# Local maxima by head groups, their queries in two transfers; a token turn one score later; half of the output product by token halves

## The chip, the cores and the metric

One Trainium2 chip, one of its cores. The metric is the device time of one execution of the whole kernel in microseconds; a kernel's time is the median of its runs. The names of the engines are those of the profile: PE (TensorE, matrix products; PEld is its loading of weights), ACT (ScalarE), DVE (VectorE), POOL (GpSimd), and SP (SyncE), which here issues the transfers. SPq is SP's queue of transfers.

## What is computed

The input is x of 8 batches x 1024 tokens x 256 channels. It is normalized over the channels (no weights), and two branches of it are added to x:

```
xn  = layernorm(x)
out = x + attention(xn) + ffn(xn)

attention: q, k, v = xn @ w_qkv + b_qkv, 16 heads of 16 channels
           heads 0..3:  causal softmax over all earlier tokens
           heads 4..15: causal softmax over the last 64 tokens
           @ w_out + b_out
ffn:       Q = xn @ W_Q.T, K = xn @ W_K.T, invQ = Q @ W_inv.T, invK = K @ W_inv.T
           branch(Q, K) + alpha * branch(invQ, invK), then @ W_O.T
branch:    per expert e of 8:  (Q @ V_e) * cumsum_over_tokens(K @ W_e)
           times the softmax weight of e (a router: gelu layer, then 8 logits)
           @ U_e, + weights @ b, / (token number)
```

All inputs are float32. The kernel splits a float32 operand into a high and a low part (names ending in H and L) and multiplies three pairs, or into three bfloat16 parts for the scores.

## The kernel before

**Chunks.** The 8192 tokens are worked in 16 chunks of 512 (two to a batch; c = ch % 2 is the half of the batch). Each chunk goes through these stages on PE:

1. *Maxima and experts.* The softmax is stabilized by the greatest score of each query. Twelve local products (L865, one for each of 4 token blocks t and 3 groups of 4 heads) and 10 (c = 0) or 26 (c = 1) global ones (L879) give scores to DVE, which takes the maxima. They are woven, four at a time, into the eight expert steps: x (L731, into bank 2), c (L731, into bank 3), the products on ACT, DVE and POOL, and mix (L843), which gathers the output in banks 0 and 1. `open` (L808) starts that sum with the gate rows WT.
2. *Local attention*, `local_groups`: six units (3 head groups x 2 halves) of scores (L899, lscore), exponentials on ACT, masks on POOL, and values (L924, lav). Beside them the next chunk's tokens are turned (L749, `turn`, banks 2 and 3) and its keys, queries (parts) and hidden layer computed.
3. *Global attention*: 6 tiles (c = 0) or 14 tiles (c = 1) of scores (L938, gscore, two for each tile), exponentials (ACT L1134), masks on the diagonal (POOL L1582), and values (L958, gav). Between them stand side stages: the next chunk's gates, its values (L731 with XH as the weights, 12 products each), and `finish` (ch, 0), the first half of the output product (L969, 12 products).

An odd chunk (c = 1) therefore follows a short global stage, an even one a long stage.

**Order.** A `Plan` lists all stages once, and each engine's program walks the same list, in order, and issues its own part of each stage behind the semaphore waits. Moving a stage in the list moves it on every engine, SP's transfers included.

**The stacks.** Keys and queries are written to DRAM in three bfloat16 parts (`parts_d`) and read back in the order of the products (`STACK`: 48 rows of partitions and three times 16): KL and QS[4:] for local heads, KG and QS[0:4] for global ones. The queries' local stacks are read by stage "stacks", ch, "queries", half: with half 0 the first three of `STACK` (L1684; 576, 192 and 192 KB), with half 1 the fourth (192 KB). L865 waits for all eight local transfers of a chunk (keys and queries) by one semaphore, `local_in`. After the global stage stage "stacks", ch, "global" (L1686) reads eight transfers of 192 and 64 KB, which L879 waits for (`global_in`).

**SP's order around a chunk's start.** `add_gate_parts` lists it: gate weights to DRAM (L1724), queries half 0, wide 0 (L1760: the gate weights of an expert pair spread over the partitions, two transfers), queries half 1, the gate rows (L1733, four transfers, weight_parts), wide 1, wide 2, and the WT rows read back (L1742, three, weight_rows; they wait until the gate rows have landed). Behind it come Vs (L1695 to L1698), the global stacks, and wide 3 and later. POOL's L1600 multiplies by a wide (weigh), DVE's L1386 by c (product), which frees bank 3; ACT's L1108 and POOL's L1605 split the result for mix (PH, PL).

Of the kernel before, what the change touches and what calls it, by code (L numbers as in the profile page):

```python
# [69 lines left out]
def mixer_layer(  # L70
# [87 lines left out]
    def peak_use():  # L158
        turns["peak"] += 1
        return f"bank{(4, 5, 6, 7)[turns['peak'] % 4]}"  # L160
# [130 lines left out]
    def add_finish(ch, k):  # L291
        add("finish", ch, k, uses=[f"phl{k}"])

    def add_residual(ch):
        add("residual", ch)

# [12 lines left out]
    def add_wide(ch, j):  # L309
        add("wide", ch, j, uses=[f"wide{j % WIDE}"])  # L310

    def add_gate_parts(ch):
        add("gate_parts", ch)
        if ch:
            add("stacks", ch, "queries", 0)
        add_wide(ch, 0)
        if ch:
            add("stacks", ch, "queries", 1)
        add("weight_parts", ch)
        for j in range(1, WIDE):  # L320
            add_wide(ch, j)
        add("weight_rows", ch)

    def add_gates(ch):
# [10 lines left out]

    def peak_groups(ch):
        c = ch % NC
        order = [[(add_lpeak, ch, t, grp, peak_use())] for t in range(T) for grp in range(NL // 4)]
        gpeaks = [[(add_gpeak, ch, t, j, peak_use())] for t in range(T) for j in range(c * T + t + 1)]
        masks = [[] for _ in order + gpeaks]  # L340
        for n, ((stage, *key),) in enumerate(order + gpeaks):
            if stage is add_lpeak:
                masks[n].append((add_seed if n >= PEAKS else add_mask, key[-1], "lpeak", *key[:-1]))
            elif stage is add_gpeak and key[2] == c * T + key[1]:
                masks[n].append((add_seed, key[-1], "gpeak", *key[:-1]))
        order[-1].append((add, "found", ch, 0))
        gpeaks[2].append((add_rows, ch, 0))
        gpeaks[-1].append((add, "found", ch, 1))
        order += gpeaks
        if ch == 0:  # L350
            add_norm(1, order)
            for t in range(T):
                order[-1].append((add, "scale", 1, t))
        blocks = range(0, len(order), PEAKS)
        joined = lambda groups, n: [stage for group in groups[n:n + PEAKS] for stage in group]
        blocks = [joined(order, n) + joined(masks, n + PEAKS) for n in blocks]
        blocks[0] = joined(masks, 0) + blocks[0]
        return blocks
# [57 lines left out]
    for ch in range(CHUNKS):  # L416
# [14 lines left out]

        last_mix = [(add_mix, ch, 2 * KB - 1, part) for part in range(2)]
        if nxt:
            for k in range(DB):
                add_turn(ch + 1, k)
            side = [last_mix] + [[(add_parts, ch + 1, w, b)] for w in (1, 0) for b in range(DB)]
            side[1].append((add_rows, ch, 1))
            side += [[(add_hidden, ch + 1, 0)] + [(add, "sums", ch + 1, k) for k in range(DB)]]
            if ch + 2 < CHUNKS:
                side[-1].append((add, "load", ch + 2))  # L440
        else:
            side = experts[split:] + [last_mix]
            side[0] = side[0] + [(add_rows, ch, 1)]
        weave(local_groups(ch), side)
        scores, values = global_groups(ch)
        if not nxt:
            run(scores[0][0] + scores[0][1])
# [8 lines left out]
        if nxt:  # L456
            first_x, first_c = ([(add, ch + 1, 0, part) for part in range(2)] for add in (add_x, add_c))
            run(first_x + scores[0][0] + scores[0][1] + first_c)
            add("logits", ch + 1, uses=["bank7"])
            add("chigh", ch, 0)  # L460
            if ch + 2 < CHUNKS:
                add_norm(ch + 2, values)
            side = [[(add_gates, ch + 1), (add, "crest", ch, 0)], [(add_gate_parts, ch + 1)]] + [[]] * (3 * (ch % NC))
            side += [[(add_values, ch + 1, 0)], [(add_values, ch + 1, 1)], [(add_finish, ch, 0)]]
        else:
            side = [[(add, "chigh", ch, 0), (add, "crest", ch, 0)], [(add_finish, ch, 0)]]

# [31 lines left out]
    with ctx:  # L499
# [130 lines left out]
        peak_in = [sem(f"peak_in{i}") for i in range(2)]  # L630
        raw_in = [sem(f"raw_in{i}") for i in range(5)]
        tok_done, turned, xhi, xlo, carried, chi, clo = (sem(n) for n in ("tok_done", "turned", "xhi", "xlo", "carried", "chi", "clo"))
        parts_ps, part1, part3, local_in, global_in, kept = (sem(n) for n in ("parts_ps", "part1", "part3", "local_in", "global_in", "kept"))
        values_ps, vs_in, vs_zero, hidden_ps = (sem(n) for n in ("values_ps", "vs_in", "vs_zero", "hidden_ps"))
        gate_max, gate_exp, rows_cast, rows_out, rows_in, opened = (
            sem(n) for n in ("gate_max", "gate_exp", "rows_cast", "rows_out", "rows_in", "opened"))
# [88 lines left out]
        def tensor_program(e):  # L725
# [12 lines left out]
            for stage in plan.stages:  # L738
# [115 lines left out]
                elif kind == "lpeak":  # L854
                    ch, t, grp = key
                    i, = where[stage]
                    q.wait_ge(local_in, 128 * (ch + 1))
                    q.wait_ge(kept, ch + 1)
                    if stage in laid:
                        q.wait_ge(seeded, nth("seed", *stage))  # L860
# [102 lines left out]

                elif kind == "finish":
                    ch, k = key[:2]
                    q.wait_ge(ctx_lo, nth("crest", *key))
                    for t in range(T) if key[2:] == () else range(2 * key[2], 2 * key[2] + 2):
                        for a, b in ((PH, OH), (PH, OL), (PL, OH)):
                            ins = e.matmul(out_half(t), a[:, k, t * P:(t + 1) * P], b[:, k, :], start=False,  # L969
# [59 lines left out]
        def scalar_program(e):  # L1029
            q = Seq(e)  # L1030

            for stage in plan.stages:
# [67 lines left out]
                elif kind == "product":  # L1100
# [3 lines left out]
                    if j >= 2:  # L1104
                        q.wait_ge(phl_read[h], use(f"phl{h}", "mix", ch, j - 2, 1))
                    elif ch:
                        q.wait_ge(phl_read[h], use(f"phl{h}", "finish", ch - 1, h))
                    e.activation(PH[:, h, :], prod[:, j % 3, :], ACT.Copy).then_inc(phi)  # L1108

                elif kind == "seed":  # L1110
# [498 lines left out]
        def sync_program(e):  # L1609
# [5 lines left out]
            for stage in plan.stages:  # L1615
# [40 lines left out]
                elif kind == "parts_out":  # L1656
                    ch, w = key
                    q.wait_ge(part1, nth("parts", ch, w, DB - 1))
                    q.wait_ge(part3, nth("parts", ch, w, DB - 1))
                    q.wait_ge(local_in, 128 * ch)  # L1660
                    q.wait_ge(global_in, 128 * ch)
                    e.dma_start(parts_d[w].rearrange("(b p) i t -> p i b t", p=P), parts[:, w, :, :, :]).then_inc(parts_out[w], 16)

                elif kind == "stacks":
# [10 lines left out]
                    for w in (0,) if reach == "queries" else (1,) if reach == "local" and ch else (1, 0):  # L1675
                        q.wait_ge(parts_out[w], 16 * (ch + 1))
                        by_head = parts_d[w].rearrange("(h d) i t -> d i h t", d=HD)
                        for rows, i in STACK if half is None else (STACK[:3], STACK[3:])[half]:
                            if i is None:
                                src = parts_d[w].rearrange("(h d) i t -> (d i) h t", d=HD)  # L1680
                            else:
                                src = by_head[:, i[1 - w], :, :]
                            if reach != "global":
                                e.dma_start(KL[rows, :, WINDOW:] if w else QS[rows, NG:, :], src[:, NG:, :]).then_inc(local_in, 16)  # L1684
                            else:
                                e.dma_start(KG[rows, :, c * C:(c + 1) * C] if w else QS[rows, 0:NG, :], src[:, 0:NG, :]).then_inc(global_in, 16)  # L1686

# [71 lines left out]
                        n = 2 * (j % KB) + k  # L1759
                        e.dma_start(wide[j % WIDE][R * k:R * (k + 1), :].rearrange("p (h t) -> p h t", h=2), by_half[n:n + 1].to_broadcast([R, 2, HALF])).then_inc(wide_in[j % WIDE], 16)  # L1760

                elif kind == "finish" and key[2:]:
                    ch, _, h = key
                    q.wait_ge(bank_read[h], use(f"bank{h}", "open", ch))
                    e.dma_start(outr[ch // NC, ch % NC, :, 2 * h:2 * h + 2], xt[:, 2 * h:2 * h + 2, :]).then_inc(stored, 16)
# [43 lines left out]
```

## Time and profile before

| | before |
|---|---|
| median of 3 runs | 1412.46 us (1409.79 to 1415.1) |
| the profiled execution | 1412.41 us |
| its span, first to last instruction | 1410.7 us |
| mean granted TensorE clock | 0.993 |
| busy share of the span | PE 96%, DVE 70%, ACT 55%, POOL 42% |
| PE's first instruction | at 11.8 us |

The span is what the trace covers; the execution's own time is 1.7 us more. In the lists by time a row gives the start, the busy time of a run of equal instructions, the engine, the line and the operation as output<-inputs, how many (x), and in brackets the idle time of the engine before it with what ended it. The waits list sums such idle time by the instruction that waited and by what it waited for.

### The profile page before, as it was taken

The numbers are of one execution on the slowest core, as the hardware profiler recorded it, in microseconds if no ns is written. First come the engines' busy times: TensorE is split into PE (matmuls) and PEld (weight loads), VectorE is DVE, ScalarE is ACT, GpSimd is POOL, SyncE is SP. The second block draws the span as 40 slices with busy tenths as digits, with TensorE's granted clock in tenths as the row PEclk, the third lists the DMA queues.
The fourth block names the chain that finished last, engine by engine and source line by source line (L and its number), as shares of the span: only waits on it lengthen the run. The fifth ranks groups of instructions, "written<-read, shape, count | busy, mean of one in ns | idle before, by whom it ended". The sixth has DMA issues, their size and how long they took to land.

```text
span 1410.7 us, 35955 instructions
## 1 busy us (share of the span) xinstructions
PE 1349.5 (96%) x14481; PEld 1022.5 (72%) x14481; DVE 986.1 (70%) x2084; ACT 773.2 (55%) x1369; POOL 594.7 (42%) x666
## 2 busy tenths in 40 slices
PE   5989999999999999999999999999999999999997
PEld 4567686777858787587867878587785868678673
DVE  6566786678856787577875778577885678757662
ACT  3434637464564746646385554747457463755544
POOL 2234443453434444354434534344452435345351
PEclk9999999999999999999999999999999999999998
DMA  9430725417172551716354181733617164351620
GB/s 241 82 95 22 170 76 138 120 60 183 41 172 75 122 142 60 170 34 166 97 127 120 47 195 40 171 90 100 160 41 187 40 155 109 102 137 48 166 61 16
DMA packets 184294, 154.45 MB, mean 109 GB/s; under 512 B 37569, under 2 KB 183872, under 8 KB 184128
## 3 DMA queue, kind: packets, MB, share of 16 engines
q1 hardware_dynamic: 183616, 151.90, 42.9%
q8 instruction: 114, 1.87, 0.6%
q14 instruction: 52, 0.43, 0.1%
q10 hardware_dynamic: 512, 0.26, 0.1%
HBM read 108.57 MB, written 37.22 MB: 103 GB/s over the span
## 4 chain that ended last, share of the span: by engine, by line
PE 75%; DVE 7%; DMA 6%; ACT 4%; POOL 3%; issue 3%; SPq 2%; POOLq 0%; ACTq 0%; DVEq 0%
PE PS L731 36%; PE PS L843 11%; PE PS L879 5%; PE PS L938 4%; DMA rest<-weights_d 3%; PE PS L924 3%; PE PS L958 3%; PE PS L865 2%; PE PS L899 2%; PE PS L969 2%; PE PS L1024 2%; DMA weights_d<-weights_t 2%; ACT HE L1126 1%; PE PS L795 1%; DVE prod L1386 1%
## 5 line engine op out<-in xcount | busy, mean ns | idle before, releaser
L1605 POOL TENSOR_TENSOR PL<-prod,PH 128x512 fp32r<-128x512 f32 x128 | 167.7, 1310 | 177.5 <-ACT PH L1108 175.0
L731 PE MATMUL PS<-XH,WH 128*128 128x512 f32 x512 | 218.4, 427 | 4.6 <-DVE rest L1259 1.8
L1108 ACT ACTIVATE PH<-prod 128x512 fp32r<-128x512 f32 x128 | 80.9, 632 | 257.4 <-DVE prod L1386 253.0
L1600 POOL TENSOR_TENSOR prod<-prod,rest 128x512 f32<-128x512 f32 x96 | 124.1, 1292 | 206.3 <-DMA rest<-weights_d 132.1
L1310 DVE TENSOR_REDUCE block_peak<-PS 128x4 f32<-128x512 f32 x288 | 179.7, 684 | 38.9 <-PE PS L879 38.7
L731 PE MATMUL PS<-XH,WL 128*128 128x512 f32 x512 | 203.8, 398 | 0.0
L731 PE MATMUL PS<-XL,WH 128*128 128x512 f32 x512 | 203.3, 397 | 0.0
L1134 ACT ACTIVATE HE<-PS 128x512 f32<-128x512 f32 (+1 forms) x320 | 163.5, 552 | 34.1 <-PE PS L938 28.7
L1582 POOL TENSOR_SCALAR_AFFINE_SELECT HE<-HE 128x256 f32<-128x256 f32 x128 | 51.4, 410 | 252.4 <-ACT HE L1134 250.6
L1386 DVE TENSOR_TENSOR prod<-PS,prod 128x512 f32<-128x512 f32 x128 | 87.5, 683 | 80.4 <-PE PS L731 61.1
L843 PE MATMUL PS<-UH,PH 128*128 128x256 f32 x512 | 133.6, 294 | 0.0
L1098 ACT ACTIVATE prod<-PS 128x512 f32<-128x512 f32 x128 | 75.5, 590 | 105.9 <-PE PS L731 94.3
L1303 DVE TENSOR_REDUCE peak<-PS 128x4 f32<-128x512 f32 x192 | 119.1, 682 | 14.4 <-PE PS L865 13.5
L843 PE MATMUL PS<-UL,PH 128*128 128x256 f32 x512 | 128.2, 283 | 0.0
L731 PEld LDWEIGHTS PS<-XH,WH 128*128 128x128 f32 x512 | 96.9, 189 | 35.6 <-issue 5.8
L1418 DVE STREAM_TRANSPOSE craw<-PS 128x512 f32<-128x512 f32 x63 | 44.7, 709 | 102.7 <-PE PS L958 91.2
L938 PE MATMUL PS<-area 99*128 99x256 bf16 (+1 forms) x640 | 110.0, 268 | 6.0 <-ACT HE L1134 5.3
L731 PE MATMUL PS<-CH,WH 128*128 128x512 f32 x256 | 108.4, 423 | 7.1 <-DVE prod L1386 7.0
L731 PEld LDWEIGHTS PS<-XH,WL 128*128 128x128 f32 x512 | 96.7, 189 | 22.6
L731 PEld LDWEIGHTS PS<-XL,WH 128*128 128x128 f32 x512 | 97.8, 191 | 14.8
L1126 ACT ACTIVATE HE<-PS 128x512 f32<-128x512 f32 x192 | 104.3, 597 | 3.1 <-PE PS L899 2.5
L938 PEld LDWEIGHTS PS<-area 99*128 99x128 bf16 x640 | 39.6, 98 | 89.3 <-ACT HE L1134 56.5
(193 smaller groups left out, 3084.3 us busy)
## 6 DMA issues: line engine op xcount, KB each, us to landing
parts_d<-area SPq DMA_DIRECT2D x32, 768.0 KB, 4.9
area<-parts_d SPq DMA_DIRECT2D x128, 192.0 KB, 6.2
rest<-weights_d SPq DMA_DIRECT2D x192, 128.0 KB, 3.6
area<-parts_d SPq DMA_DIRECT2D x32, 576.0 KB, 6.8
tok<-in_L_attn_x_dram SPq DMA_DIRECT2D x16, 512.0 KB, 6.2
xt<-in_L_attn_x_dram SPq DMA_DIRECT2D x16, 512.0 KB, 4.6
wide<-weights_d SPq DMA_DIRECT2D x64, 128.0 KB, 3.6
out_dram<-xt SPq DMA_DIRECT2D x15, 512.0 KB, 4.4
```

The source lines that it names most:

```text
L731: ins = e.matmul(ps, a, b, start=first and k == 0, stop=last and k == n - 1, skip_group_check=True)
L843: ins = e.matmul(out_half(t), (PH, PL)[part][:, h, t * P:(t + 1) * P], u[:, j, :], start=False, stop=False, skip_group_check=True)
L938: ins = e.matmul(psum(i, lo=HALF * a + lo, hi=HALF * (a + 1)), KG[0:KSTK, g, j * P:(j + 1) * P], QS[0:KSTK, g, half * HALF + lo:(half + 1) ...
L1098: e.activation(prod[:, j % 3, :], psum(i), ACT.Copy).then_inc(bank_read[i])
L1108: e.activation(PH[:, h, :], prod[:, j % 3, :], ACT.Copy).then_inc(phi)
L1126: e.activation(HE[:, k, :], psum(i), ACT.Exp, scale=SCALE).then_inc(bank_read[i])
L1134: e.activation(two(HE[:, k, :], lo), two(psum(i), lo), ACT.Exp, scale=SCALE).then_inc(bank_read[i])
L1303: e.tensor_reduce(peak[:, t, 4 * grp:4 * (grp + 1)], psum(i).rearrange("p (a k) -> p a k", a=4), AX_X, ALU.max).then_inc(bank_read[i])
L1310: e.tensor_reduce(block_peak[ch % NC][:, t, :, j], psum(i).rearrange("p (a k) -> p a k", a=4), AX_X, ALU.max).then_inc(bank_read[i])
L1386: e.tensor_tensor(prod[:, r, :], psum(3), prod[:, r, :], ALU.mult).then_inc(bank_read[3])
L1600: e.tensor_tensor(prod[:, j % 3, :], prod[:, j % 3, :], wide[j % WIDE], ALU.mult).then_inc(weighed)
L1605: e.tensor_tensor(PL[:, j % 2, :], prod[:, j % 3, :], PH[:, j % 2, :].bitcast(F32), ALU.subtract).then_inc(plo)
```

## The change

- The twelve local maxima are ordered by head group, then token block (it was the other way round), and groups 1 and 2 wait for a semaphore of their own, `later_in`.
- The queries' local transfers are four for heads 4 to 7 and four for heads 8 to 15, where four carried heads 4 to 15. All four of the first part come ahead of wide 0, all four of the second behind it.
- Wide 1 is issued ahead of the gate rows.
- The second turn of the next chunk's tokens comes behind the first local score, no longer ahead of it.
- In the long global stages `finish` (ch, 0) is two stages of 6 products, at tiles 4 and 6, in place of 12 products at tile 12; the next chunk's values are at tiles 9 and 11 in place of 9 and 10. In all stages the pieces of the norm come a tile earlier.

```diff
+    def add_half(ch, half):
+
+        add("finish", ch, 0, half, uses=[] if half else ["phl0"])
@@ add_gate_parts
         add_wide(ch, 0)
         if ch:
             add("stacks", ch, "queries", 1)
+        add_wide(ch, 1)
         add("weight_parts", ch)
-        for j in range(1, WIDE):
-            add_wide(ch, j)
+        add_wide(ch, 2)
         add("weight_rows", ch)
@@ peak_groups
-        order = [[(add_lpeak, ch, t, grp, peak_use())] for t in range(T) for grp in range(NL // 4)]
+        order = [[(add_lpeak, ch, t, grp, peak_use())] for grp in range(NL // 4) for t in range(T)]
@@ the chunk loop
         if nxt:
-            for k in range(DB):
-                add_turn(ch + 1, k)
+            add_turn(ch + 1, 0)
...
-        weave(local_groups(ch), side)
+        units = local_groups(ch)
+        if nxt:
+            units[0].insert(1, (add_turn, ch + 1, 1))
+        weave(units, side)
...
-                add_norm(ch + 2, values)
-            side = [[(add_gates, ch + 1), (add, "crest", ch, 0)], [(add_gate_parts, ch + 1)]] + [[]] * (3 * (ch % NC))
+                add_norm(ch + 2, values[:-1])
+            side = [[(add_gates, ch + 1), (add, "crest", ch, 0)], [(add_gate_parts, ch + 1)]]
             side += [[(add_values, ch + 1, 0)], [(add_values, ch + 1, 1)], [(add_finish, ch, 0)]]
+            if ch % NC:
+                side = {0: side[0], 1: side[1], 3: [(add_half, ch, 0)], 5: [(add_half, ch, 1)], 8: side[2], 10: side[3]}
+                side = [side.get(n, []) for n in range(len(scores) - 1)]
@@ tensor_program, lpeak
                     q.wait_ge(local_in, 128 * (ch + 1))
+                    if grp:
+                        q.wait_ge(later_in, 64 * (ch + 1))
@@ tensor_program, finish
-                    q.wait_ge(ctx_lo, nth("crest", *key))
+                    q.wait_ge(ctx_lo, nth("crest", *(key if k else (ch, 0))))
@@ sync_program, stacks
-                        for rows, i in STACK if half is None else (STACK[:3], STACK[3:])[half]:
+                        for rows, i in STACK:
...
-                            if reach != "global":
-                                e.dma_start(KL[rows, :, WINDOW:] if w else QS[rows, NG:, :], src[:, NG:, :]).then_inc(local_in, 16)
+                            if reach != "global" and w:
+                                e.dma_start(KL[rows, :, WINDOW:], src[:, NG:, :]).then_inc(local_in, 16)
+                            elif reach != "global":
+                                for part in range(2) if half is None else (half,):
+                                    heads = slice(NG + 4, NH) if part else slice(NG, NG + 4)
+                                    e.dma_start(QS[rows, heads, :], src[:, heads, :]).then_inc((local_in, later_in)[part], 16)
```

The rest of the diff makes the new semaphore, lets the write of the parts wait for it too, and names the new `finish` stages where their use of PH and PL is looked up.

## Rows read from the trace of the kernel before

**Rows 1.** The page: busy time, share of the span and instructions of each engine.

```profile
PE 1349.5 (96%) x14481; PEld 1022.5 (72%) x14481; DVE 986.1 (70%) x2084; ACT 773.2 (55%) x1369; POOL 594.7 (42%) x666
```

**Rows 2.** Waits of PE: line, released by: us in total, times, longest.

```profile
PE PS L731 <- DVE prod L1386: 7.0, 9, 3.3
...
PE PS L865 <- DMA area<-parts_d: 4.8, 8, 1.2
PE PS L749 <- DVE prod L1386: 2.6, 7, 0.4
...
PE PS L879 <- DMA area<-parts_d: 0.2, 1, 0.2
```

**Rows 3.** SP's queue by time: chunk 4's stacks, chunk 5's start, chunk 15's stacks.

```profile
418.31 5.11 SPq L1686 DMA_DIRECT2D area<-parts_d  x8
...
488.18 0.34 SPq L1724 DMA_DIRECT2D weights_d<-weights_t  x1
488.56 1.89 SPq L1684 DMA_DIRECT2D area<-parts_d  x3
491.30 1.26 SPq L1760 DMA_DIRECT2D rest<-weights_d  x2
492.61 0.60 SPq L1684 DMA_DIRECT2D area<-parts_d  x1
493.31 3.03 SPq L1733 DMA_DIRECT2D rows_d<-weights_b  x4
496.38 1.27 SPq L1760 DMA_DIRECT2D rest<-weights_d  x2
497.69 2.05 SPq L1760 DMA_DIRECT2D wide<-weights_d  x2
499.85 1.90 SPq L1742 DMA_DIRECT2D WT<-rows_d  x3
...
503.27 5.20 SPq L1686 DMA_DIRECT2D area<-parts_d  x8
...
1330.99 5.23 SPq L1686 DMA_DIRECT2D area<-parts_d  x8
```

**Rows 4.** PE by time: first maxima of chunks 4, 5 and 15.

```profile
439.49 1.07 PE L879 MATMUL PS<-area 96*128 96x128 bf16 x16
...
498.44 1.08 PE L865 MATMUL PS<-area 96*64 96x128 bf16 x32 [0.56 <-DMA area<-parts_d]
499.78 0.50 PE L731 MATMUL PS<-CH,WH 128*128 128x512 f32 x1 [0.25 <-DVE prod L1386]
...
511.59 1.07 PE L879 MATMUL PS<-area 96*128 96x128 bf16 x16 [0.17 <-DMA area<-parts_d]
...
1340.00 1.07 PE L879 MATMUL PS<-area 96*128 96x128 bf16 x16
```

**Rows 5.** Issue to landing of the last two global stacks, chunks 5 and 15.

```profile
DMA to landing us min/median/max: 2.6/3.1/3.7
...
DMA to landing us min/median/max: 2.3/2.3/2.3
```

**Rows 6.** Waits of SP's queue: line, released by: us in total, times, longest.

```profile
SPq L1717 <- DMA peak_d_global<-peak_t_global: 20.4, 16, 1.9
...
SPq L1742 <- DMA rows_d<-weights_b: 1.9, 3, 1.0
```

**Rows 7.** PE by time, long global stage of chunk 3.

```profile
402.02 0.72 PE L938 MATMUL PS<-area 99*128 99x256 bf16 x4
...
403.22 0.76 PE L938 MATMUL PS<-area 99*128 99x256 bf16 x4
...
414.47 0.37 PE L969 MATMUL PS<-OH,PH 128*128 128x256 f32 x1
...
415.99 0.39 PE L938 MATMUL PS<-area 99*128 99x256 bf16 x2
```

**Rows 8.** PE by time behind the turns of chunk 5.

```profile
539.10 0.40 PE L899 MATMUL PS<-area 99*128 99x64 bf16 x8
539.34 0.38 PE L893 MATMUL PS<-mask_l,ident_b 128*128 128x512 bf16 x1
```

More of the change, by code:

```diff
@@ L632, in mixer_layer @@
         tok_done, turned, xhi, xlo, carried, chi, clo = (sem(n) for n in ("tok_done", "turned", "xhi", "xlo", "carried", "chi", "clo"))
-        parts_ps, part1, part3, local_in, global_in, kept = (sem(n) for n in ("parts_ps", "part1", "part3", "local_in", "global_in", "kept"))
+        parts_ps, part1, part3, local_in, later_in, global_in, kept = (
+            sem(n) for n in ("parts_ps", "part1", "part3", "local_in", "later_in", "global_in", "kept"))
         values_ps, vs_in, vs_zero, hidden_ps = (sem(n) for n in ("values_ps", "vs_in", "vs_zero", "hidden_ps"))
@@ L1106, in scalar_program @@
                     elif ch:
-                        q.wait_ge(phl_read[h], use(f"phl{h}", "finish", ch - 1, h))
+                        q.wait_ge(phl_read[h], use(f"phl{h}", "finish", ch - 1, h, *([0] if h == 0 and (ch - 1) % NC else [])))
                     e.activation(PH[:, h, :], prod[:, j % 3, :], ACT.Copy).then_inc(phi)
@@ L1660, in sync_program @@
                     q.wait_ge(local_in, 128 * ch)
+                    q.wait_ge(later_in, 64 * ch)
                     q.wait_ge(global_in, 128 * ch)
@@ L1760, in sync_program @@
                         e.dma_start(wide[j % WIDE][R * k:R * (k + 1), :].rearrange("p (h t) -> p h t", h=2), by_half[n:n + 1].to_broadcast([R, 2, HALF])).then_inc(wide_in[j % WIDE], 16)
-                elif kind == "finish" and key[2:]:
+                elif kind == "finish" and key[1] == 1 and key[2:]:
                     ch, _, h = key
```

## The prediction

> **What bounds the kernel now.** I read the page first: TensorE (PE) is busy in 96% of the span and no other engine comes near it [rows 1]. So a change can gain only what PE idles, some 61 us, of which 12 us lie before its first instruction; and it loses whatever makes PE idle more. Next I read PE's waits by line, because they say which idle time this change can touch: 4.8 us at the first local-maxima products (L865) for query transfers, 7.0 us at L731 for VectorE's product, 2.6 us at L749, the second turn of tokens, and almost nothing (0.2 us, once) at L879, the first global-maxima products, for the global transfers [rows 2]. Listing these waits by time shows where they stand. Chunks alternate: an odd chunk comes after a short global stage (6 tiles), an even one after a long stage (14 tiles). The L865 waits stand only at the start of the odd chunks, 0.1 to 1.2 us each, followed by 0.25 to 0.57 us at L731 in seven of them (2.7 us together); the even chunks start without a wait.
>
> Then I read the transfer queue of SyncE (SP), since every edit in it is one more instruction in an in-order queue. Around the start of chunk 5 SP issues 28 transfers from 488.2 us to 508.5 us, and after the weights have landed at 491.3 us it never pauses: wide 0 (2), the fourth query transfer, the gate rows (4), wide 1 and wide 2 (4), the WT rows (3), Vs (2), the eight global stacks [rows 3]. The reader is to see that one issue costs about 0.65 us whatever it moves: eight global ones take 5.20 us, the single 192 KB query transfer 0.60 us [rows 3]. The last global stack lands 3.7 us after its issue in chunk 5, and 2.2 to 2.4 us after it as a rule [rows 5]; in chunk 5 L879 starts at 511.59 us with a wait of 0.17 us for it, in chunk 15 it starts at 1340.00 us, 2.1 us after the landing (1330.99 + 5.23 - 0.60 + 2.3 = 1337.9) [rows 3 to 5]. The same subtraction gives the spare time of L879 in the eight odd chunks 1, 3, ... 15 as 1.5, 0.3, -0.2, 0.75, 1.35, 0.8, 1.2 and 2.1 us: 7.8 us together, one microsecond each. So in odd chunks SP's issue rate is the second bound, right behind PE. In even chunks it is not: chunk 4's stacks were issued by 423.4 us and L879 came at 439.5 us [rows 3, 4].
>
> **The change part by part.**
>
> *Queries in two parts.* Four transfers of four heads and four of eight heads replace four of twelve: the same bytes, 1152 KB, but eight issues for four. The first local maxima need only the first part and are reordered so that four products of head group 0 come first. The first part (384 KB) is issued where 960 KB were before, so it lands well before 498.4 us, and the L865 wait goes. Wide 0 is issued right behind it; with less traffic ahead of it the product that L731 waits for 0.25 us [rows 4] comes sooner, and that wait goes too. The second part is out by about 495 us and, at the 5.8 us that the fourth transfer took (492.6 to 498.4) [rows 3, 4], down by 501, before the second block of products at about 502. So 4.8 + 2.7 = 7.5 us of PE waits go ahead of L879.
>
> Against it stands the queue. Behind wide 0 SP now issues four query transfers, not one: 3 x 0.65 = 1.95 us more in each odd chunk before the global stacks. The fourth transfer of the first part goes into the time in which SP waited for the weights anyway (490.45 to 491.30 in chunk 5 [rows 3]); in chunks 9 and 15 SP did not wait there and pays 0.6 us. Sum over eight chunks: 15.6 + 1.2 = 16.8 us.
>
> *Wide 1 before the gate rows.* Before, the gate rows were followed by four wide issues (2.6 us) that covered their landing, which the WT rows need. Now only two cover it: the WT issue comes 0.67 + 1.30 = about 2.0 us after the last rows issue starts. SP waited for that landing three times, 1.9 us together and 1.0 at most [rows 6]; in those cases it took 3.4 to 4.4 us, in the thirteen others less than some 3.4. Nearest lower bound: the maxima's transfers to the same memory, for which SP waits 20.4 us / 16 = 1.3 us after the last issue [rows 6], so 0.6 + 1.3 = 1.9 us. The new wait is then 0 to 2.0 us; with 2.65 us (the middle of 1.9 and 3.4) thirteen times and 3.7 three times it is 0.8 us on average, which I take: 6.4 us in eight chunks. Chunk 0 has the same reorder at its first L808, which already waits for WT: between -0.4 and +0.9, I take +0.4 us. Wide 1 itself comes 3.0 - 1.95 = 1.1 us earlier; POOL waits for it, PE does not.
>
> SP is thus late by 16.8 + 6.4 = 23.2 us in sum; the spare time is 7.8 us; L879 starts later by 23.2 - 7.8 = 15.4 us in sum than now. This is measured against SP's clock, so the 7.5 us saved ahead of L879 do not come off: PE gets there sooner and waits longer. L808 (WT) is late by the same amount but has 1 to 2 us more spare time or the same, and lies on the same path. Behind L879, wide 3 and wide 4 are issued after the stacks and are late by as much; the multiplication by wide 3 and the PL behind it on POOL fed the products of j=2 1.3 us before they were needed in chunk 5 (516.0 against 517.3 us), where L879 had -0.2, so they follow and add nothing. Even chunks have 14 us of spare time and pay nothing.
>
> One rule bears on this. The row above shows 0.6 to 0.65 us of SP for each transfer from 64 KB to 576 KB. The Trainium skill, "DMA: Bandwidth & Descriptors", Rules for kernel authors, says to join many small transfers into one, as under 64 KB one pays mostly overhead. The new parts are 64, 128, 192 and 384 KB, so by that threshold the split would cost nothing and the sum would be lower by 16.8 us; the trace says that the cost is in the number of issues, not in the size.
>
> *Second turn one score later.* In seven odd chunks the second turn waits 0.37 us (2.6 us together) for bank 3 [rows 2]. The score put before it takes 0.24 us from its start to the next instruction's (539.10 to 539.34) [rows 8] and needs no bank that VectorE still holds: it ran without a wait directly after. It fills the wait: -0.24 x 7 = -1.7 us. ScalarE's XH of the second turn comes 0.55 us later, the first exponential 0.55 earlier; XL and the scans have about 1 us before the keys' products need them. Bound: 0 to -2.6.
>
> *Output product's first half by token halves.* In seven long stages 12 products move from the last tile but one to the 4th and 6th as 6 + 6. Without side work a tile takes 1.24 us from start to start (402.02 to 403.22 and its neighbours) though PE has work for 1.10: the two exponentials pace it [rows 7]. Before, 12 products took 1.52 us (414.47 to 415.99) [rows 7]. Now each half adds 0.72 + 0.09 for the changeover and takes back about 0.25 of that idle time in its tile and the next: +1.1 us for two. At the end of the stage, from tile 10, I laid out the scores, exponentials, diagonal masks and values by their durations: 8.23 us with both values and finish inside become about 6.9 (the 1.52 leave, 0.2 of new waiting for masks comes, as tile 12 now has no cover). Net -0.2 us each, -1.4 in all; bounds -0.6 to +0.3 each. The norm pieces move one tile forward on VectorE, which idles 11 us there: nothing.
>
> **Sum**: +15.4 + 0.4 - 1.7 - 1.4 = +12.7 us on the profiled execution's 1412.41 us (span 1410.7 and 1.7 around it), which is the median of the runs, 1412.46, for all purposes. Forecast 1425.1 us, slower by 0.9%.
>
> **The rivals.** (1) *The queue recovers part of it.* From wide 0 to the last stack, chunk 5 took 16.6 us for 23 issues, and at the plain rates of its rows about 15.6; others took 16.2 to 17.1. A single wide pair took 2.05 us for 1.3 [rows 3]. If smaller transfers end such long issues (0.9 x 8 = -7.2) and the gate rows land in 2 us (-6.4), the time is 1411.5; with one of the two, 1418 to 1419. For it: nothing shows what lengthens an issue. Against it: one of the long ones coincides with POOL's multiplication, not with a large transfer. The fixed cost of about 2.0 us that the Trainium skill gives in the same page, Anatomy of one DMA, would mean the second of the two; here only unloaded transfers come near it.
> (2) *Faster: the queue does not bind.* If the stacks land at most 1 us later, L879 does not move and the removed waits count: -4.8 - 2.7 - 1.7 - 1.4 = -10.6, so 1401.8 us. It decides from a delay of one microsecond in SP; for it speaks only that L879 hardly waits now.
> (3) *Slower still*: rows land in 4 us each time, +9.6 us: 1434.7.
>
> **How the numbers follow.** The forecast's own case, 1419 to 1432, gets 0.58; the third rival 0.04; the first 0.23; the second 0.15. A measurement of this kernel tells 0.5% (7.1 us) from no change, so slower is above 1419.5: 0.60; within: 0.24; faster, below 1405.4: 0.16. The range reaches from 1405, where most of the second rival is left out, to 1433.
>
> **What would show it.** Right: no wait at L865 at the start of odd chunks; SP's last global stack issued 2 to 4 us later after the weights' transfer than 19.7 us (488.18 to 507.86); PE waits at L808 and L879 of 15.4 + 7.5 = about 23 us in sum for DMA; nothing new in even chunks; finish at tiles 4 and 6 and tile-12 and -13 waits for POOL at or above 0.28 us. The forecast is wrong if L879 waits under 1 us per odd chunk, if an issue of the halved transfers takes clearly under 0.6 us, or if POOL's multiplication by wide 2 or wide 3 becomes what PE waits for.

## The result, and the profile after

The changed kernel takes 1422.59 us (median of 6 runs, 1421.05 to 1424.04) against 1414.18 us of the kernel before on the same chips. The ratio is 1.0065, 95% interval 1.0049 to 1.0080: slower by about 9 us, by less than the forecast 12.7. The profiled execution has a span of 1422.3 us for 1410.7. Of the 24 runs of the experiments 10 and 11 below three took 2108 to 3203 us, for a reason that is not known, and no ratio counts them.

First the page after (busy time, as in [rows 1]): PE's busy time is 1.1 us less (DVE's 5.2 more), so the 11.6 us are waits.

```profile
PE 1348.4 (95%) x14481; PEld 1024.1 (72%) x14481; DVE 991.3 (70%) x2084; ACT 774.9 (54%) x1369; POOL 592.4 (42%) x666
```

Then PE's waits, which answer to [rows 2]. The lines have moved: L808 is L818 now, L865 L877, L879 L891, L731 L741, L899 L911, L938 L950, L958 L970.

```profile
PE PS L818 <- DMA WT<-rows_d: 14.2, 8, 3.0
...
PE PS L950 <- ACT HE L1146: 8.7, 32, 2.1
PE PS L741 <- DVE prod L1398: 7.1, 7, 3.3
PE PS L891 <- DMA area<-parts_d: 4.6, 6, 1.6
PE PS L970 <- POOL HE L1594: 4.6, 16, 0.3
PE PS L877 <- ACT PS L1126: 2.8, 7, 1.0
...
PE PS L911 <- ACT PS L1131: 1.8, 8, 0.2
```

The wait of the first maxima for the queries and the one at the second turn are gone, 7.4 us. In their place PE waits 14.2 us for WT (2.4 before, in chunk 0 alone; it is 3.0 there now, so 11.2 in the odd chunks) and 4.6 us for the global stacks.

SP's queue around the start of chunk 5 shows why. It answers to [rows 3]:

```profile
489.42 0.34 SPq L1741 DMA_DIRECT2D weights_d<-weights_t  x1
489.80 2.48 SPq L1701 DMA_DIRECT2D area<-parts_d  x4
492.69 1.26 SPq L1777 DMA_DIRECT2D rest<-weights_d  x2
493.99 2.56 SPq L1701 DMA_DIRECT2D area<-parts_d  x4
496.59 1.26 SPq L1777 DMA_DIRECT2D rest<-weights_d  x2
497.95 3.04 SPq L1750 DMA_DIRECT2D rows_d<-weights_b  x4
501.04 1.87 SPq L1777 DMA_DIRECT2D wide<-weights_d  x2
503.01 1.89 SPq L1759 DMA_DIRECT2D WT<-rows_d  x3
...
506.42 5.80 SPq L1703 DMA_DIRECT2D area<-parts_d  x8
```

A halved transfer costs what a whole one costs: four in 2.56 us where one took 0.60. The issues of WT end 15.5 us after the start of the weights' transfer (13.6 before), and the last stack is issued at 506.42 + 5.80 - 0.60 - 489.42 = 22.2 us (19.7 before). PE by time in the same chunk, as in [rows 4]:

```profile
499.05 1.08 PE L877 MATMUL PS<-area 96*64 96x128 bf16 x32
...
507.83 0.61 PE L818 MATMUL PS<-bias_rows,WT 99*128 99x256 bf16 x4 [2.05 <-DMA WT<-rows_d]
...
510.12 1.92 PE L877 MATMUL PS<-area 96*64 96x128 bf16 x32
...
515.26 1.07 PE L891 MATMUL PS<-area 96*128 96x128 bf16 x16
```

and from issue to landing, the last two stacks of this chunk, as in [rows 5]:

```profile
DMA to landing us min/median/max: 2.6/3.1/3.6
```

The last stack is issued at 511.6 us and lands 3.6 us later, at 515.2, and L891 starts at 515.26. It is so in all eight odd chunks: L891 starts 0.05 us after the last stack's landing, where L879 before started 0.05 to 2.06 us after it. So it is the landing of the stacks that sets how long the start of an odd chunk takes, also in chunks 5 and 11, where no wait stands at L891: there PE had waited at L818 before, on the way.


The products at 510.12 take 1.92 us where they took 1.08, and no wait stands beside them. The windows of that stretch tell what it is (columns: stretch, its length, busy time of PE, PEld, DVE, ACT, POOL with instructions, then the granted clock, DMA share, GB/s):

```profile
506.00:509.00 3.00, 1.17 (x11) 1.14 (x12) 1.97 (x4) 2.79 (x5) 2.28 (x2) 1.00 0.80 210
509.00:511.00 2.00, 2.00 (x26) 1.78 (x26) 0.20 (x1) 0.12 (x1) 0.00 (x0) 0.58 0.41 115
511.00:513.00 2.00, 2.00 (x23) 1.69 (x20) 2.00 (x4) 0.00 (x0) 0.00 (x0) 0.56 0.55 168
```

After the idle stretch the granted clock was at the lower of its two levels (1.2 for 2.4 GHz) for some 3.4 us. It did not delay L891, which the last stack released.

To weigh the parts against each other I measured in every profile the same intervals between starts of PE's instructions. In sums: from the first mask product of an odd chunk (L851) to its first global maximum, 8 chunks, 116.7 us before and 131.3 after (+14.6); local stage, from the first turn to the first global score, odd chunks 166.8 and 166.4, even ones 162.5 and 161.4 (together -1.5); the seven long global stages 184.9 and 185.5 (+0.6). The even chunks' starts take 17.68 us before and after, each of them.

### The profile page after: what moved, and what is told of

It is laid out like the page before. It is cut to its first block, busy times and chain, and to the rows that moved or that the text cites. A ratio compares the mean times of both kernels' runs of the same rounds, so it can differ in the third digit from the quotient of the medians.

```text
span 1422.3 us, 36035 instructions
## 1 busy us (share of the span) xinstructions
PE 1348.4 (95%) x14481; PEld 1024.1 (72%) x14481; DVE 991.3 (70%) x2084; ACT 774.9 (54%) x1369; POOL 592.4 (42%) x666
## 3 DMA queue, kind: packets, MB, share of 16 engines
q8 instruction: 114, 1.87, 0.5%
## 4 chain that ended last, share of the span: by engine, by line
PE 69%; SPq 11%; DVE 7%; issue 4%; ACT 4%; DMA 3%; POOL 2%; ACTq 0%; POOLq 0%; DVEq 0%
PE PS L741 34%; PE PS L853 10%; PE PS L891 5%; PE PS L950 3%; PE PS L936 3%; PE PS L970 3%; SPq L1701 3%; SPq L1777 2%; PE PS L911 2%; PE PS L1036 2%; SPq L1703 2%; SPq L1750 2%; PE PS L981 2%; PE PS L877 2%; ACT HE L1146 2%
## 5 line engine op out<-in xcount | busy, mean ns | idle before, releaser
L741 PE MATMUL PS<-XH,WH 128*128 128x512 f32 x512 | 218.3, 426 | 4.4 <-DVE rest L1271 1.8
L741 PE MATMUL PS<-XH,WL 128*128 128x512 f32 x512 | 203.7, 398 | 0.0
L741 PE MATMUL PS<-XL,WH 128*128 128x512 f32 x512 | 203.2, 397 | 0.0
L741 PEld LDWEIGHTS PS<-XH,WH 128*128 128x128 f32 x512 | 96.8, 189 | 35.0 <-issue 5.0
L950 PE MATMUL PS<-area 99*128 99x256 bf16 (+1 forms) x640 | 109.9, 268 | 10.0 <-ACT HE L1146 8.7
L741 PE MATMUL PS<-CH,WH 128*128 128x512 f32 x256 | 108.4, 423 | 7.1 <-DVE prod L1398 7.1
L741 PEld LDWEIGHTS PS<-XH,WL 128*128 128x128 f32 x512 | 96.7, 189 | 22.8
L741 PEld LDWEIGHTS PS<-XL,WH 128*128 128x128 f32 x512 | 97.6, 191 | 14.8
L950 PEld LDWEIGHTS PS<-area 99*128 99x128 bf16 x640 | 39.9, 98 | 90.1 <-ACT HE L1146 51.2
```

The source lines that it names most:

```text
L741: ins = e.matmul(ps, a, b, start=first and k == 0, stop=last and k == n - 1, skip_group_check=True)
L950: ins = e.matmul(psum(i, lo=HALF * a + lo, hi=HALF * (a + 1)), KG[0:KSTK, g, j * P:(j + 1) * P], QS[0:KSTK, g, half * HALF + lo:(half + 1) ...
```

## The experiments

Each ran with the kernel before on the same chip; a ratio is that of the runs, with its 95% interval.

**1. The split alone** (with the order of the maxima that it needs; wide 1 behind the gate rows as before).

```diff
-        order = [[(add_lpeak, ...)] for t in range(T) for grp in range(NL // 4)]
+        order = [[(add_lpeak, ...)] for grp in range(NL // 4) for t in range(T)]
...
-    for rows, i in STACK if half is None else (STACK[:3], STACK[3:])[half]:
+    for rows, i in STACK:      # heads 4..7 with half 0, heads 8..15 with half 1
```

> The kernel before with the queries in two parts and the local maxima by head group alone (wide 1 behind the gate rows as before, turn and finish as before). Theory (number of issues): SP's last global stack comes about 2.4 us later after the weights' transfer in each odd chunk (about 22.1 us for 19.7), L808 and L879 wait for transfers by about 16 us in sum, the waits at L865 are gone, and the time is 10 to 12 us above the kernel before (ratio 1.007 to 1.009). Rival (it is the new order of wide 1 and the gate rows that makes WT late, since the largest wait after the change is at the first use of WT): without that order WT is in time, and the removed waits make the kernel 5 to 7 us faster (ratio 0.995 to 0.997).

1429.15 us, ratio 1.0120 (1.0102 to 1.0138). The rival falls: the split alone costs more than the whole change. It costs more than my theory too. Waits of PE in its profile, over all chunks:

```profile
PE PS L809 <- DMA WT<-rows_d: 11.6, 7, 3.1
...
PE PS L868 <- ACT PS L1117: 5.0, 12, 2.3
```

Chunk 3, first POOL, then DVE, then PE (start, busy time, and the idle time before):

```profile
341.82 1.28 POOL L1603 TENSOR_TENSOR prod<-prod,rest 128x512 f32<-128x512 f32 x1 [5.31 <-DMA rest<-weights_d]
```

```profile
343.14 0.69 DVE L1389 TENSOR_TENSOR prod<-PS,prod 128x512 f32<-128x512 f32 x1 [2.91 <-POOL prod L1603]
...
344.94 2.47 DVE L1306 TENSOR_REDUCE peak<-PS 128x4 f32<-128x512 f32 x4
```

```profile
340.32 1.08 PE L868 MATMUL PS<-area 96*64 96x128 bf16 x32
345.01 0.61 PE L809 MATMUL PS<-bias_rows,WT 99*128 99x256 bf16 x4 [2.01 <-DMA WT<-rows_d]
...
347.94 1.65 PE L868 MATMUL PS<-area 96*64 96x128 bf16 x32
```

The multiplication by wide 1 waits 5.31 us for its transfer, which stands behind the three more query transfers and the gate rows. DVE takes its instructions in order: with the product it holds back the maxima of the block at 340.32, finished already, and ACT can't lay the next masks until they are through. PE's waits at L868 for masks are 5.0 us (2.2 before). The 1.65 us of the products at 347.94 are mostly no wait: the granted clock is at its lower level from about 346 to 349 us. In six of the eight odd chunks the first global maxima (L882) start 0.3 to 1.9 us after their last stack has landed, so here WT and the chain behind wide 1 set the time, and no longer the stacks.

From the weights' transfer to POOL's start on wide 1 it takes 12.6 us in the mean before, 15.3 here, and 13.5 in the changed kernel, where wide 1 goes ahead of the gate rows. So the swap, which the prediction booked as pure cost, takes back about 0.4% beside the split (1.0120 less the turn's 0.12%, against 1.0065; each with an interval of some 0.2% either way). The profiles show 2.4 us of it in the odd chunks' starts (133.7 us here, 131.3 in the changed kernel) and 2.7 us in chunk 0, and the lower clock takes part in both (one stretch more here in the starts, two more in chunk 0). How much of it is wide 1 alone stays open.

**2. Wide 1 first alone.**

> The kernel before with wide 1 ahead of the gate rows alone. Theory: SP waits a few microseconds in sum for the gate rows to land, but less than the spare time of L879 and L808 (7.8 us in eight odd chunks, 1 us each), so the time stays within 2 us of before (ratio 0.999 to 1.001); L808 waits at most 1 us more in chunk 0. Rival (the order is the cost): 6 to 9 us slower (ratio 1.004 to 1.006), with waits at L808 in the odd chunks.

1416.49 us, ratio 1.0024 (1.0013 to 1.0035). Neither expectation: a small cost, but not at L808. The odd chunks' starts take 122.4 us for 116.7.

```profile
PE PS L865 <- DMA area<-parts_d: 6.7, 8, 1.3
...
PE PS L865 <- ACT PS L1114: 4.2, 19, 0.8
PE PS L808 <- DMA WT<-rows_d: 3.4, 1, 3.4
```

The first maxima wait 6.7 us for the queries (4.8 before; 2.7 to 4.3 in runs 3 to 6, which leave wide 1 where it was), and 4.2 us for masks (2.2). A part of it is that the last query transfer is now in flight beside wide 1: it takes 6.1 us to land for 5.9, 1.7 us in eight chunks. SP waits 8.5 us in ten chunks for the gate rows to land (1.9 in three before): with two issues behind them and not four, they are seldom down in time.

**3. The turn alone.** The diff is the one shown with the change.

> The kernel before with the second turn behind the first local score alone. Theory as predicted: the 2.6 us at the turn go and 1.7 us are won (ratio 0.9988). Rival read from the profile after (the idle time moves to the next score at L899, which waits for the mask that ACT copies, 0.2 us each): at most 0.5 us from the odd chunks and 1.2 us from the even ones (ratio 0.999). Both are at the edge of what can be told; the waits by line decide.

1410.95 us, ratio 0.9988 (0.9976 to 1.0000). The wait at the turn goes, and 1.8 us come at the next score (here L901), eight times 0.2:

```profile
PE PS L901 <- ACT PS L1121: 1.8, 8, 0.2
```

The intervals give -0.4 us in the odd chunks and -1.2 in the even ones, where there was no wait to fill. The size was right and the place was not. In all fourteen stages the first exponential now goes ahead of the second XH on ACT; that this is the gain is probable, but no run separates it.

**4. The halves alone** (with the values and the norm pieces moved as in the change).

> The kernel before with finish by halves at tiles 4 and 6, the values at tiles 9 and 11 and the norm a tile earlier alone. Prediction: 1.4 us faster (ratio 0.999). Reading of the profile after: the long global stage takes 26.50 us for 26.41, so 0.6 us slower in seven stages (ratio 1.0004), with 3.4 us more of waits at L938 for ACT's exponentials and 1.2 us less at L958 for POOL.

1412.95 us, ratio 1.0002 (0.9991 to 1.0014): nothing that can be told. The long stages take 185.5 us for 184.9 and the waits are those of the changed kernel:

```profile
PE PS L945 <- ACT HE L1141: 8.7, 32, 2.1
...
PE PS L965 <- POOL HE L1589: 4.3, 15, 0.3
```

**5. Three tiny transfers.** 512 bytes each, from the input to a scratch row, behind wide 0 in the kernel before.

```diff
+    for _ in range(3 if half == 1 else 0):
+        e.dma_start(tiny_d[n:n + 1, :], x[0, n:n + 1, 0:128]).then_inc(tiny_in, 16)
```

> The kernel before with three more transfers of 512 bytes each (from the input to a scratch row that nobody reads) on SP right behind wide 0, ahead of the fourth query transfer; everything else as before, the local maxima in their old order. Theory (the cost is the number of issues in SP's queue): wide 1, the WT rows and the global stacks are all 1.9 us later in each chunk, the odd chunks take 1 to 2 us more each as in the run with the split alone (17 us slower there, with 2 us of late issues and wide 1 late), so 10 to 16 us slower (ratio 1.007 to 1.011), and more than that as the fourth query transfer is 1.9 us late too and L865 waits for it. Rival (what delays is the traffic of the added and moved transfers, not their number): 1.5 KB move nothing, ratio 1.000 to 1.002.

1421.65 us, ratio 1.0071 (1.0053 to 1.0089). The rival falls: 1.5 KB per chunk cost 10 us.

```profile
492.36 1.26 SPq L1766 DMA_DIRECT2D rest<-weights_d  x2
493.66 1.86 SPq L1682 DMA_DIRECT2D tiny_d<-in_L_attn_x_dram  x3
495.57 0.62 SPq L1690 DMA_DIRECT2D area<-parts_d  x1
```

Three issues of 512 bytes take 1.86 us, and POOL starts on wide 1 14.6 us after the weights' transfer for 12.6. The odd chunks' starts take 125.4 us for 116.7. Against my expectation the waits at L865 did not grow (4.1 us): what is late is wide 1 and, behind DVE, the masks (L866 waits 4.7 us for ACT), as in the first run.

The Trainium skill's rule of the prediction ("DMA: Bandwidth & Descriptors", Rules for kernel authors: join small transfers, under 64 KB one pays mostly overhead) sets a threshold that these issues don't show: on SP 512 bytes and 384 KB cost the same, so joining saves queue time above 64 KB too.

**6. The order of the maxima alone.**

> The kernel before with the local maxima by head group alone, still behind all eight transfers. Theory: the order costs and gains nothing, ratio 0.999 to 1.001. Rival (the new order delays DVE's or ACT's part in it): over 1.003, with more waits at L865 for ACT's masks.

1410.42 us, ratio 0.9991 (0.9981 to 1.0001). It costs nothing.

**7 and 8. The second query part on ACT's queue**, in odd chunks, where ACT idled 3.5 us; in the eighth run with wide 1 first. Neither has the halves.

```diff
+    if nxt and (ch + 1) % NC:      # behind the last values of the short stage, on ACT
+        add("later", ch + 1)       # 4 x e.dma_start(QS[rows, 8:16, :], ...).then_inc(later_in, 16)
```

> The change without the wide order and without the halves (split, order of the maxima, turn), and with the four transfers of the second query part issued by ACT in the odd chunks, behind the last exponential of the short global stage, where ACT idled 3.5 us; SP keeps them in the even chunks. Theory: SP issues one transfer less behind wide 0 than before in odd chunks, so neither wide 1 nor WT nor the global stacks are late; the waits at L865 (4.8 us), part of those at L731 and 1.7 us of the turn are won: 5 to 9 us faster than before (ratio 0.9935 to 0.9965), L808 and L879 wait for nothing but chunk 0's 2.4 us. Rival (the second part lands too late for the second block of maxima, or ACT's issues delay its copy of x): waits at L865 for transfers of 1 us or more in each odd chunk, ratio 1.000 or above.

> As the run with the second part on ACT, with wide 1 ahead of the gate rows as in the change. Theory: wide 1 is then 3.6 us earlier than before, POOL and DVE wait less in the odd chunks, and the WT rows have the spare time that the missing issue gives back: within 2 us of the run with the old order (ratio 0.993 to 0.9975). If the swap alone costs what it cost beside the old transfers (0.24%) it is 3 us slower than that run.

1421.59 us, ratio 1.0066 (1.0046 to 1.0085), and 1421.68 us, 1.0073 (1.0058 to 1.0088). This was a real miss. In the odd chunks WT is no longer waited for, as expected, and the stacks only in the eighth run (1.9 us in three chunks); but c's product is. The run with the old order:

```profile
PE PS L736 <- DVE prod L1402: 17.7, 10, 3.3
```

Its transfers from 484 to 500 us (KB each, median time to landing):

```profile
rest<-weights_d SPq DMA_DIRECT2D x4, 128.0 KB, 5.3
area<-parts_d ACTq DMA_DIRECT2D x1, 384.0 KB, 5.8
area<-parts_d ACTq DMA_DIRECT2D x3, 128.0 KB, 6.2
wide<-weights_d SPq DMA_DIRECT2D x2, 128.0 KB, 4.9
```

The transfers of wide 0 alone in chunk 5, in this run and then in the changed kernel:

```profile
DMA to landing us min/median/max: 4.3/5.3/6.2
...
DMA to landing us min/median/max: 3.1/3.7/4.3
```

On SP the 768 KB of the second part are issued behind wide 0; on ACT they are issued beside it and share the sixteen DMA engines with it. The changed kernel issues the same transfers up to wide 0, so it is the one to compare with: over the eight odd chunks the transfers of wide 0 take 5.4 us to land for its 4.0, and POOL starts on wide 0 10.4 us after the weights' transfer for 8.9. In the kernel before they took 5.7 us, behind 960 KB of queries, but were issued 0.6 us earlier, and POOL started at 9.7. PE, freed of its waits at the first maxima, comes earlier than before and waits for the product 13.4 us in the odd chunks (2.7 before). SP waits 8.4 us for the gate rows (20.0 in the eighth run). The profiled execution is the fastest of the six (1416.52 us), so it shows less than the whole cost. So the rival of the fifth run is half true: bytes cost as well, where they are in flight beside a transfer that something waits for. The Trainium skill says this in the same page, Issuing engines are not separate DMA queues: transfers started by any engine run on the same 16 DMA engines and interleave, and a second issuer saves only the time of issuing. By that rule, the trace agrees: the changed kernel's 4.0 us became 5.4.

**9 and 10. The gate rows on ACT's queue.** 48 KB in four transfers leave SP in the odd chunks; all large ones stay in SP's order. Split, order, wide 1 first and turn as in the change, no halves; in the tenth run wide 1 stands ahead of the second query part too.

```diff
-        add("weight_parts", ch)
+        if not ch % NC:
+            add("weight_parts", ch)
...
+        if nxt and (ch + 1) % NC:
+            add("act_rows", ch + 1)    # the same four transfers, issued by ACT
```

> The change without the halves (split, order of the maxima, wide 1 first, turn), with the four gate-row transfers (48 KB together) issued by ACT in the odd chunks, behind the last exponential of the short global stage, in place of SP. All large transfers stay in SP's order. Theory (SP's issues are the cost, and little data on a second queue disturbs nothing): SP's last global stack comes about 18 to 19 us after the weights' transfer (before 19.7, change 22.5), L808 and L879 wait for nothing in the odd chunks, the L865 waits stay gone, and the kernel is 5 to 9 us faster than before (ratio 0.994 to 0.9965). Rival (traffic, not issues: the second query part ahead of wide 1 delays what follows in any case): no better than 0.998, with c's product (L731) or L808 waiting.

> As the run with the gate rows on ACT, with wide 1 also ahead of the second query part. Theory: POOL's multiplication by wide 1 starts near 12 us after the weights' transfer (13.5 in the change, 12.6 before), and the second query part lands near 13.5 us after it, just when the second block of maxima wants it: within 2 us of the run with the gate rows on ACT; waits at the second L865 for transfers of up to 1 us per odd chunk if it is late.

1411.21 us, ratio 0.9987 (0.9978 to 0.9996), and 1411.38 us, 0.9985 (0.9974 to 0.9997). Both beat the kernel before, by less than I expected, and the changed one by some 11 us. The ninth run's waits:

```profile
PE PS L737 <- DVE prod L1403: 7.5, 7, 3.3
...
PE PS L873 <- ACT PS L1131: 3.3, 14, 0.8
PE PS L814 <- DMA WT<-rows_d: 3.0, 2, 2.9
```

In the ninth run no global maximum waits for its stacks and WT is late in chunk 0 alone, but for 0.2 us; L814 waits another 1.0 us in chunk 5, put down to DVE. What is missing to 5 us is in part that SP now waits for the rows (9.5 us in ten chunks), so the last stack is issued at 20.0 us, no earlier than before, and that c's product is still waited for (3.3 us in the odd chunks). The odd chunks' starts take 118.7 and 117.9 us, still no less than the 116.7 before: the gain over the kernel before is no larger than the turn's alone. In the tenth run the second part was late in six chunks (5.2 us at L873), as its expectation allowed, and WT in four odd ones (2.8 us).

**11. All but the split.**

> The change with the queries' transfers as before (three ahead of wide 0, one behind, all eight waited for), everything else as in the change. Theory: SP's queue is as short as before, the sum of the single runs (wide 1 first +0.24%, turn -0.12%, halves 0, order 0) holds: ratio 1.000 to 1.002, waits at L808 and L879 in the odd chunks under 2 us in sum. Rival (wide 1 first is itself what makes WT late): ratio 1.004 or more with waits at L808.

1416.95 us, ratio 1.0025 (1.0015 to 1.0034), a little above the expected range. WT is waited for in chunk 0 alone (2.2 us), the rival falls. 1.0065 less 1.0025 leaves 0.4% for the split, in this company.

**12. The gate rows on ACT without the split.**

> The kernel before with the turn one score later and the gate rows on ACT in the odd chunks (so SP goes wide 0, fourth query transfer, wide 1, wide 2, WT), without the split and in the old order of the maxima. It tells what the split is worth where SP's queue has room. Theory (the split takes 5 to 7 us of waits at L865 and L731 when it costs no time in the queue): this run keeps the waits at L865 of 4 to 7 us and is 2 to 5 us slower than the run with the split and the rows on ACT (ratio to before 1.000 to 1.002). Rival (the split moves the waits elsewhere even then): ratio 0.998 to 0.999, as with the split.

1417.77 us, ratio 1.0031 (1.0018 to 1.0043). It differs from the ninth run by the split and the order alone (the order is worth nothing, run 6) and is slower by 0.44%: with the gate rows off SP's queue the split is worth 6 us. Without the split, the rows on ACT together with wide 1 first are a loss of 0.4% against the turn alone (run 3): SP waits 28.3 us for the gate rows, and the last stack is issued at 19.6 us, no earlier than before. Its first maxima wait 6.9 us for the queries:

```profile
PE PS L870 <- DMA area<-parts_d: 6.9, 7, 2.1
```

That is not all of the 6 us. The odd chunks' starts take 122.2 us for the ninth run's 118.7, and from the first global maximum to the turn they take 4.1 us more (186.5 for 182.4), which is in part waits for masks at the global maxima (1.2 us) and otherwise stays open. The profile is of the slowest of the twelve runs, 5 us above their median.

## Why the prediction was right

The direction, the mechanism and the place were as forecast: slower by the issue rate of SP, in the odd chunks alone, and the first global maxima start 0.05 us after their last stack in each of them. That the sum came so near is in part luck: terms that were too large and terms that were left out nearly cancel. One of the prediction's own signs of being wrong even appeared: L891 waits under 1 us per odd chunk (4.6 us in eight). It was a bad sign, since PE spends most of its waiting at L818 on the way there; the start of L891 against the landing decides. By its terms:

- *SP late by 23.2 us in sum.* Measured 22.39 - 19.67 us in the mean of eight odd chunks, 21.8 us. The three more issues behind wide 0 are some 16 to 17 of it, near the forecast 15.6: the four of the second part take 2.77 us in the mean, the one before took 0.68 (run 5 shows that it is their number). The fourth transfer of the first part was booked at 1.2 us and the start of wide 0 is 3.4 us late in sum: more chunks than two had no wait there to hide it in. With the 0.6 us of the next term about 1 us is left, in issues that ran longer in one kernel than in the other.
- *The gate rows' landing, 6.4 us.* This is the term of the sum that was mis-sized. SP waits for them 2.5 us after the change and 1.9 before, so 0.6. The pair of issues of wide 2 was itself long in four of the eight chunks (1.87 us for 1.26 in chunk 5), which gave the rows time. In run 2, where it was long once, the wait did grow, to 8.5 us; why the pair runs long is not known, so this term came out small by luck.
- *Later start of L879, 15.4 us.* Measured 14.6. The lower clock in chunk 5 is no part of it, since the stack released L891 there as well. 11.2 of the 15.8 us of waits stand at L818 although WT had more spare time than the stacks, as the prediction says: WT's last issue comes 3.0 us later in the mean (the stacks' 2.7), PE, without its waits at the first maxima, comes 0.1 to 1.0 us earlier, and L818 is the first of the two that it reaches. The sum of both waits was to be 23 us and is 15.8. Of the 7.1 us between, 0.8 are the smaller delay; 2.7 are c's product, which was forecast to come early enough and is still waited for, 2.8 us in the odd chunks (POOL starts on wide 0 0.75 us earlier, but PE comes earlier too); 0.7 are waits for masks; and in 2.9 PE's own pieces take longer, 1.7 of it lost to the lower clock.
- *"Wide 1 itself comes ... 1.1 us earlier; POOL waits for it, PE does not"*: its last issue starts 0.5 us earlier, but its transfers take 4.9 us to land for 3.5, in flight beside the second query part, so it lands 0.9 us later. The rest is wrong as a rule. In the changed kernel it is nearly so; in runs 1 and 5, where wide 1 is 2 to 3 us late, DVE passes the wait on to PE, and run 1 costs 17 us. The swap of wide 1 was counted as a cost of 6.4 us; alone it costs 0.24% (3.4 us), beside the split it takes back some 0.4% (run 1). So the split was booked too cheap and the swap too dear, and the two errors cancel in the sum.
- *The turn, -1.7 us*: measured -1.5, most of it from another place (run 3).
- *The halves, -1.4 us*: measured +0.6. The two tiles cost +1.1 as laid out; from tile 9 to the end 12.68 us were needed for 13.69, a gain of 1.0 and not 1.3, with new waits of 0.25 and 0.27 us for exponentials at tiles 10 and 12. The step that failed there is that the tail's new waits were counted for masks alone.
- *Chunk 0, +0.4 us*: 0.55 at L808, but the chunk as a whole was 1.9 us shorter in this profile. Its length from the first global maximum to the local stage differs by over 2 us between profiles, below.

The measured time lies between the prediction's own sum, 1425.1 us, and the first rival (part of the delay taken back): without the rows' term the sum is 1418.7 us. That rival's condition held in part, as the rows cost only 0.6 us; the long issues did not go away, as it also allowed. The second, faster, needed SP late by no more than 1 us; runs 9 and 10 made that true by other means, and even there the starts of the odd chunks did not get shorter. The fixed cost of about 2.0 us that the prediction takes from the Trainium skill ("DMA: Bandwidth & Descriptors", Anatomy of one DMA) is fitted there to transfers that GpSimd issues; the gate rows are issued by SP, and no run here times their landing by itself.

## What to carry to other kernels

Count a queue's issues before its bytes: a transfer split in two takes twice the time of its in-order queue, and what is late is whatever stands behind it, here gate rows and global stacks that nobody had touched. A wait that is small in the trace may be held small by two chains that end together; taking one away wins nothing until the other has room, so measure the spare time of the second before editing the first. When issues move to another engine's queue, move the small transfers: here large ones, in flight beside a transfer that something waits for, cost as much as the issues they saved.

## What the runs showed of the hardware

An issue on SP took 0.60 to 0.65 us for 512 bytes as for 384 KB. It is not one number for every transfer, but not the size either: the gate rows, 12 KB each, took 0.67 to 0.82 us, the weights, 128 KB, 0.34. About one issue in twenty took 0.9 us and more, up to 2.0 in run 1, without a cause that the profile shows; what lengthens them stays open.

The granted clock fell to its lower level in the middle of the changed kernel, from about 509 to 513 us, behind a wait of 2.05 us at L818, while 2.19 us in chunk 9 did not bring it down. Most profiles have such stretches in chunk 0, where PE idles several times: none in the tenth run, one to four of 3.4 us in the others. They account for how chunk 0's second half (from the first global maximum to the turn) differs between the fourteen profiles: 22.9 us in the five without such a stretch in it, 24.1 to 24.5 in the five with one, 25.3 in the four with two. From 118 to 125.5 us, the kernel before (two) and the tenth run (none), in the columns named above:

```profile
118.00:125.50 7.50, 5.85 (x23) 5.27 (x24) 2.29 (x6) 1.26 (x2) 2.56 (x2) 0.54 0.02 3
...
118.00:125.50 7.50, 5.93 (x55) 5.53 (x55) 3.63 (x8) 3.59 (x7) 3.70 (x4) 1.00 0.03 5
```

So one stretch at the lower clock costs 1.1 to 1.5 us there, and a difference of 1 to 2 us between two single profiles of this kernel is no sign of a change. That the spread between the runs of one kernel is the same thing is probable but not shown.
